# Attention block over 64 graphs: first group normed on VectorE, two-step weight scales, 11 warming matmuls, another order ahead of the loop

## The reference

```python
# x: 64 graphs x 128 tokens x 384, adj: 64 x 128 x 128 booleans, 6 heads of 64
h = jnp.maximum(_layernorm(x, axis=-1), 0.0)          # (x - mean) / sqrt(var + 1e-5), then ReLU
q, k, v = (_heads(h @ W + b) for W, b in ((Wq, bq), (Wk, bk), (Wv, bv)))
scores = jnp.einsum('bhqd,bhkd->bhqk', q, k) / np.sqrt(64)
bias = jnp.where(adj, 0.0, -9e15)[:, None]
probs = jax.nn.softmax(scores + bias, axis=-1)
ctx = jnp.einsum('bhqk,bhkd->bhqd', probs, v)
return x + ctx.transpose(0, 2, 1, 3).reshape(x.shape) @ Wf + bf
```

## Time and profile before

| | us |
|---|---|
| median of 3 runs | 475.55 |
| lowest, highest | 475.0, 476.55 |
| span of the profiled execution | 473.5 |
| PE busy, share of the span | 461.8, 98% |
| DVE, ACT, POOL busy | 369.9, 366.1, 303.6 |

### The profile page before, as it was taken

How to read it: one execution, slowest core, us unless ns; L and a number is a source line. 1 busy time by engine, 2 the same in 40 slices (tenths; PEclk the granted TensorE clock), 3 DMA queues, 4 the chain that set the end, 5 groups by cost and what they waited for, 6 DMA issues and landing times.

```text
span 473.5 us, 12912 instructions
## 1 busy us (share of the span) xinstructions
PE 461.8 (98%) x4457; PEld 273.0 (58%) x4457; DVE 369.9 (78%) x746; ACT 366.1 (77%) x820; POOL 303.6 (64%) x307
## 2 busy tenths in 40 slices
PE   7989999999999999999999999999999999999996
PEld 3645556556465565746556475665646556464763
DVE  5988979868888696886869688695987788687954
ACT  4879898876887887877788787788878877876950
POOL 3376767777678565767756576765667577533852
PEclk9999999999999999999999999999999999999999
DMA  8153959989979797896959679694969979776995
GB/s 302 61 118 90 162 112 169 187 182 215 187 138 225 118 194 175 184 199 124 215 123 213 155 156 214 130 213 80 217 147 164 239 120 163 184 108 150 150 192 162
DMA packets 219615, 78.56 MB, mean 166 GB/s; under 512 B 199472, under 2 KB 219568, under 8 KB 219568
## 3 DMA queue, kind: packets, MB, share of 16 engines
q1 hardware_dynamic: 209200, 65.63, 71.0%
q10 hardware_dynamic: 10368, 12.33, 9.6%
HBM read 16.19 MB, written 12.58 MB: 61 GB/s over the span
## 4 chain that ended last, share of the span: by engine, by line
PE 80%; DVE 6%; SPq 5%; issue 2%; POOL 2%; DMA 2%; ACT 2%; ACTq 0%; POOLq 0%; DVEq 0%
PE ps_proj L995 23%; PE ps_proj L997 22%; PE ps_proj L996 22%; PE ps_scores L1060 7%; SPq L565 2%; PE ps_ctx L995 2%; SPq L557 2%; PE ps_ctx L996 2%; PE ps_ctx L997 2%; PE ps_proj L1123 1%; DMA ht_parts<-h_pairs 1%; DMA ct_parts<-ctx_parts 1%; DVE shift_by L820 1%; POOL probs_parts L637 1%; DVE stats L807 1%
## 5 line engine op out<-in xcount | busy, mean ns | idle before, releaser
L637 POOL TENSOR_TENSOR probs_parts<-probs,probs_parts 128x768 f16<-128x768 f32 x64 | 105.3, 1646 | 35.2 <-ACT probs_parts L751 35.0
L736 ACT ACTIVATE probs<-masked,neg_max 128x128 f32<-128x128 f32 x384 | 118.5, 389 | 8.0 <-DVE neg_max L867 6.7
L995 PE MATMUL ps_proj<-ht_parts,w_hi 128*128 128x512 f16 (+1 forms) x309 | 109.8, 361 | 1.7 <-DVE qkt_lo L839 0.8
L996 PE MATMUL ps_proj<-ht_parts,w_hi 128*128 128x512 f16 (+1 forms) x309 | 109.7, 360 | 0.0
L997 PE MATMUL ps_proj<-ht_parts,w_lo 128*128 128x512 f16 (+1 forms) x309 | 109.7, 360 | 0.0
L720 ACT ACTIVATE qkt_hi<-ps_proj,bias_qk 128x512 f16<-128x512 f32 x94 | 63.6, 680 | 40.5 <-PE ps_proj L997 39.9
L643 POOL TENSOR_TENSOR ctx_parts<-ctx_sb,ctx_parts 128x384 f16<-128x384 f32 x62 | 56.9, 918 | 52.1 <-ACT ctx_parts L757 51.9
L839 DVE SCALAR_TENSOR_TENSOR qkt_lo<-ps_proj,bias_qk,qkt_hi 128x512 f16<-128x512 f32 x94 | 68.7, 740 | 22.0 <-ACT qkt_hi L720 22.0
L858 DVE SCALAR_TENSOR_TENSOR masked<-ps_scores,score_unscale,mask 128x384 f32<-128x384 f32 x128 | 72.5, 609 | 8.4 <-PE ps_scores L1060 8.4
L622 POOL TENSOR_TENSOR h_pairs<-h_sb,h_pairs 128x384 f16<-128x384 f32 x60 | 54.5, 917 | 37.6 <-ACT h_sb L711 37.5
L632 POOL TENSOR_TENSOR x_bf<-x_sb,b_out 128x384 f32<-128x384 f32 x64 | 63.1, 999 | 5.2 <-DVE y_sb L890 3.9
(11 more groups left out here) (102 smaller groups left out, 918.5 us busy)
## 6 DMA issues: line engine op xcount, KB each, us to landing
y<-y_sb SPq DMA_DIRECT2D x64, 192.0 KB, 2.6
x_sb<-in_x ACTq DMA_DIRECT2D x56, 192.0 KB, 3.2
x_sb<-in_x SPq DMA_DIRECT2D x8, 192.0 KB, 5.6
pt_parts<-probs_parts SPq DMA_TRANSPOSE x64, 4.0
ct_parts<-ctx_parts SPq DMA_TRANSPOSE x62, 3.0
adj_sb<-in_adj ACTq DMA_DIRECT2D x14, 64.0 KB, 2.8
w_raw<-in_Wk SPq DMA_DIRECT2D x1, 576.0 KB, 6.2
w_raw<-in_Wv SPq DMA_DIRECT2D x1, 576.0 KB, 7.3
```

Of the source, the lines that this page charges most:

```text
L637: nc.gpsimd.tensor_tensor(probs_parts[b][:, 1, :], probs[b % 2][:], probs_parts[b][:, 0, :], ALU.subtract).then_inc(probs_split, 1)
L736: last = nc.scalar.activation(probs[b % 2][:, u * N:(u + 1) * N], masked[b % 2][:, u, :], ACT.Exp, bias=neg_max[b % 2][:, u:u + 1])
L995: nc.tensor.matmul(to, a_hi, b_hi, start=first, stop=False)
L996: nc.tensor.matmul(to, a_hi, b_lo, start=False, stop=False)
```

## The change

- Group 0 is normed by DVE: one `tensor_scalar` per graph, (x - mean) * rstd in float32, SBUF to SBUF, in place of `first_shift` on DVE and `normalize_first` on ACT. The ReLU moves behind the transpose: `first_hi` takes `Relu` for `Copy`, and `first_lo` becomes a `scalar_tensor_tensor` (max with 0, minus hi). These instructions count on a semaphore of their own, `first_h_ready`.
- `scale` has two steps: the bound and the factor 1/1024 move into `sum_rows`, whose matrix holds 1/1024 and which adds one more matmul of a tiny constant (2 to the -100).
- `keep_busy` makes 11 matmuls at the start, not 15.
- All turns below 40000 are new, on all engines. The loop and what follows it keep their order. A few places of it:
  - DVE, start: statistics 0, reduce_bias, first_moments 0, reduce_first_rows 0 to 2, statistics 1, normalize_first 0, first_moments 1, scale 0, statistics 2 and 3, normalize_first 1, weight_rest 0, first_moments 2 and 3, first_lo 0, scale_bias 0, reduce_rows 0, normalize_first 2 and 3, weight_rest 1 and 2, first_lo 1, scale 1, reduce_rows 1, first_lo 2 and 3, statistics of group 1, scale 2, weight_rest 3, aggregate 1, weight_rest 4 to 6, shift 1, weight_rest 7 and 8, scale_bias 1, qk_lo 0, reduce_rows 2, score_unscale, additive_mask 0, qk_lo 1 to 3, scale 3, qk_lo 4 and 5, output_bias, values_lo 0 to 2, mask_scores 0, largest_score 0, mask_scores 1, statistics 2.0, largest_score 1, statistics 2.1 to 2.3, aggregate 2, values_lo 3, statistics 3.0 and 3.1, additive_mask 1, qk_lo 1.0.
  - PE, start: keep_busy, sum_rows 0, turn_first 0 and 1, keep_busy, keep_busy, turn_first 2, sum_rows 1, turn_first 3, first_q 0 and 1, sum_rows 2, first_q 2 and 3, project_qk 3 and 4, project_v 0, sum_rows 3, project_qk 5, project_v 1, project_bias, project_v 2, scores 0, project_v 3, project_qk 1.0 to 1.3, scores 0.1. Before: keep_busy, sum_rows 0, turn_first 0, keep_busy twice, turn_first 1, first_q 0, sum_rows 1, turn_first 2, first_q 1, sum_rows 2, turn_first 3, first_q 2 and 3, project_qk 3 to 5, sum_rows 3, project_v 0, project_bias, project_v 1 and 2, scores 0, project_v 3.
  - ACT: weight_hi 0 and 1, first_hi 0 and 1, weight_hi 2, first_hi 2 and 3, weight_hi 3 and 4, bias_term 0 to 2, weight_hi 5 to 8, qk_hi 0 and 1, normalize 1.0, qk_hi 2 and 3, normalize 1.1 to 1.3, qk_hi 4 and 5, values_hi 0 to 2; then the loads of x of groups 2 and 3 between exponentials.

```diff
-SCALE_STEPS = 3
+SCALE_STEPS = 2
-KEEP_BUSY = (15, 4, 3)
+KEEP_BUSY = (11, 4, 3)
...
-                nc.vector.tensor_scalar(w_bound[:, at], row_sum(n), TINY, 1.0 / ROWS_MOST, ALU.max, ALU.mult)\
-                    .then_inc(scale_step, 1)
+                nc.vector.tensor_scalar(w_unscale[:, at].bitcast(I32), row_sum(n).bitcast(I32), EXPONENT_BITS,
+                                        None, ALU.bitwise_and).then_inc(scale_step, 1)
                 dve.wait_ge(scale_step, before + 1)
-                nc.vector.tensor_scalar(w_unscale[:, at].bitcast(I32), w_bound[:, at].bitcast(I32), EXPONENT_BITS,
-                                        None, ALU.bitwise_and).then_inc(scale_step, 1)
-                dve.wait_ge(scale_step, before + 2)
                 nc.vector.reciprocal(w_scale[:, at], w_unscale[:, at]).then_inc(scale_step, 1)
...
-            def first_shift(group, n, i):
-                dve.wait_ge(rstd_ready, n + 1)
-                shift_graphs(0, first_parts[n])
+            def normalize_first(group, b, i):
+                at = slice(b, b + 1)
+                dve.wait_ge(rstd_ready, b + 1)
+                nc.vector.tensor_scalar(h_sb[:, b, :], x_sb[0][:, b, :], moments[0][:, b, 0:1], rstd[0][:, at],
+                                        ALU.subtract, ALU.mult).then_inc(first_h_ready, 1)
...
-                nc.vector.tensor_tensor(lo, first_turned(b), hi, ALU.subtract).then_inc(first_h_split, 1)
+                nc.vector.scalar_tensor_tensor(out=lo, in0=first_turned(b), scalar=0.0, in1=hi, op0=ALU.max,
+                                               op1=ALU.subtract).then_inc(first_h_split, 1)
...
+                nc.tensor.matmul(row_sum(n), parts_of_one[:], tiny[:], start=True, stop=False)
+                if n < 2:
+                    nc.tensor.matmul(row_sum(n), parts_of_one[:], bias_rows[:, n:n + 1], start=False, stop=False)
                 for c in range(C):
-                    last = nc.tensor.matmul(row_sum(n), ones[:], w_rows[:, n, c:c + 1], start=c == 0,
-                                            stop=n >= 2 and c == C - 1)
-                if n < 2:
-                    last = nc.tensor.matmul(row_sum(n), ones[:], bias_rows[:, n:n + 1], start=False, stop=True)
+                    last = nc.tensor.matmul(row_sum(n), parts_of_one[:], w_rows[:, n, c:c + 1], start=False,
+                                            stop=c == C - 1)
```

More of the change, by code:

```diff
@@ L66 @@
     0: {
[L67 to L82, removed]
-        "reduce_first_rows": (38390, 38400, 38420), "reduce_rows": (38570, 38610, 38780), "reduce_bias": (38430,),
@@ L126 @@
-    3: {
-        "load": (9090, 9100, 9200, 9210), "load_mask": (9400,), "statistics": (9110, 9210, 9240, 9290),
-        "aggregate": (9300,), "inverse_deviation": (9620,), "shift": (9310,), "normalize": (9320, 9410, 9420, 9430),
-        "normed_lo": (9650, 9680, 9710, 9720), "transpose_normed": (9740, 9760),
-        "project_qk": (9740, 9760, 9780, 9790, 9820, 9860), "qk_hi": (9600, 9620, 9650, 9670, 9720, 9790),
-        "qk_lo": (9600, 9670, 9680, 9710, 9760, 9800), "project_v": (9870, 9920, 9930, 9980),
-        "values_hi": (9830, 9880, 9930, 9960), "values_lo": (9830, 9900, 9940, 10223), "additive_mask": (9440,),
-        "residual": (9830, 9930, 9950, 9970), "scores": (9900, 9940), "mask_scores": (9840, 9850, 9910, 9990),
-        "largest_score": (9880, 9930, 9950, 10570), "exponentials": (9870, 9940, 9970, 12387),
-        "probs_hi": (9920, 9980, 11692, 14668), "probs_lo": (9980, 10460, 12021, 14997),
-        "transpose_probs": (9990, 11094, 12655, 15631),
-    },
@@ new lines @@
+        "qk_hi": (38760, 38770, 38790, 38800, 38840, 38850), "qk_lo": (38790, 38830, 38840, 38850, 38870, 38880),
+        "project_v": (39330, 39360, 39380, 39400), "values_hi": (38860, 38870, 38880, 38960),
+        "values_lo": (38900, 38910, 38920, 39020), "additive_mask": (38820,),
+        "residual": (39410, 39420, 39430, 39440), "scores": (39390, 39450),
+        "mask_scores": (38930, 38950, 39110, 39120), "largest_score": (38940, 38970, 39140, 39150),
+        "exponentials": (38980, 39020, 39180, 39190), "probs_hi": (39050, 39080, 39220, 39260),
@@ new lines @@
+    3: {
+        "load": (9000, 9010, 9070, 9250), "load_mask": (9200,), "statistics": (9030, 9040, 9130, 9270),
+        "aggregate": (9280,), "inverse_deviation": (9610,), "shift": (9310,), "normalize": (9360, 9370, 9380, 9450),
+        "normed_lo": (9660, 9670, 9700, 9720), "transpose_normed": (9720, 9770),
+        "project_qk": (9740, 9750, 9780, 9790, 9800, 9850), "qk_hi": (9600, 9640, 9680, 9690, 9710, 9770),
+        "qk_lo": (9600, 9620, 9690, 9710, 9780, 9790), "project_v": (9870, 9920, 9930, 9970),
+        "values_hi": (9810, 9840, 9880, 9940), "values_lo": (9840, 9890, 9900, 10223), "additive_mask": (9730,),
+        "residual": (9930, 9940, 9960, 9970), "scores": (9910, 9950), "mask_scores": (9850, 9870, 9920, 9980),
+        "largest_score": (9860, 9880, 9930, 10570), "exponentials": (9850, 9930, 9990, 12387),
+        "probs_hi": (9890, 9980, 11692, 14668), "probs_lo": (9950, 10460, 12021, 14997),
+        "transpose_probs": (9960, 11094, 12655, 15631),
+    },
```

151 lines of the change are left out of this document (84 added, 67 removed).

## The result

The changed kernel takes 472.34 us at the median of 13 executions (470.98 to 475.01), the kernel before 475.4 in the 13 between them: ratio 0.9932, 95% interval 0.9918 to 0.9946, so 3.1 us faster where 1.7 were forecast. The profiled span falls from 473.55 to 469.73 us.

| | first scores | first scores of the loop | last scores | end |
|---|---|---|---|---|
| before | 31.97 | 134.54 | 442.92 | 473.55 |
| after | 30.10 | 130.65 | 438.64 | 469.73 |
| difference | -1.87 | -3.89 | -4.28 | -3.82 |

A forecast was written before the change was run, and what follows sets the result against it. PE, 98% busy, was taken to bound the kernel. Terms of -2.16 us on DVE and PE's walk put the first scores 2.0 us earlier; 0.3 given back leaves -1.7: span 471.8, plus 2.05 around it, 473.85 us, range 472.3 to 475.9.

The forecast's parts named there:

- 0.3 given back: PE from the first scores to the loop: new gaps cost 0.3 us of the early gain, bounds -0.47 and +1.9.
- Scale in two steps: DVE ahead of the first scores: one dependent step of 0.19 us fewer, four times, -0.76 us.
- `first_shift` gone: DVE ahead of the first scores: four small independent instructions fall away, -0.3 us.
- The norm: DVE ahead of the first scores: four new norms, 0.35 us busy, a step of 0.27 each, +1.1 us, at most +1.85.
- `first_lo`: DVE ahead of the first scores: scalar_tensor_tensor at 611 ns against tensor_tensor at 551, four times, +0.24 us.
- The wait for the sums: DVE at the start: its 0.98 us idle for PE's weight row sums shrinks to about 0.1, -0.9 us.
- The shift of group 1: DVE ahead of the first scores: 0.94 us falls to 0.15 without POOL work beside it, -0.8; wait of 0.38 stays.
- The mask: DVE: additive_mask 1 moves behind the first scores, half of the two masks' 1.47 us, -0.74 us.
- PE beside it: PE's start walked: products from 12.5 us, 17.2 us of work, 0.2 of seams, first scores at 29.95 us.
- Given back behind the scores: Rival: behind the first scores, a late load of x makes DVE and PE 1.9 us late; 475.45 us, chance 0.22.
- The norm waiting for POOL: Rival: at the start, one DVE norm slowed by POOL beside it costs 0.75 us more; 474.6 us, chance 0.07.
- The clock: Rival: at PE's start the rise to 2.4 GHz comes late, half-rate work costs 3.25 us; 477.1 us, chance 0.09.

The follow-up runs named there:

- late_order: Kernel before with its own order up to the first scores and the changed kernel's order from there to the loop; 473.4 us, ratio 0.9942.
- three_steps_b: Changed kernel with scale back in three steps, second measurement; 471.61 us, ratio 0.9930.
- warm15: Changed kernel with 15 warming matmuls at the start in place of 11; 473.5 us, ratio 0.9940.
- before_warm11: Kernel before with 11 warming matmuls at the start in place of 15; 473.8 us, ratio 0.9985.
- after_again: Changed kernel itself, unedited, measured a second time; 472.51 us, ratio 0.9940.
- after_third: Changed kernel itself, unedited, measured a third time; 472.14 us, ratio 0.9924.
- early_only: Changed kernel with the order of the kernel before from the first scores to the loop; 475.05 us, ratio 0.9977.
- three_steps_end: Changed kernel with scale back in three steps and its extra buffer allocated behind all others; 473.08 us, ratio 0.9942.
- warm_no_second: Changed kernel without the 4 and 3 later warming matmuls; 474.19 us, ratio 0.9989.
- pad16: Changed kernel with an unused buffer of 16 bytes per partition and no added instruction; 472.09 us, ratio 0.9926.
- three_steps: Changed kernel with scale back in three steps, first measurement; 471.66 us, ratio 0.9906.

## Why the prediction was right, and where it was wrong

**What bounds it.** PE, before and after: right. That PE's idle time from 32.0 to 117.7 us was 0.47 us: this is the step that failed, and with it the term "0.3 given back", which starts from it; they carry the whole miss. The 0.47 was read off busy time, whose modelled ends hide up to 0.16 or 0.17 us of every hole, and the cut at 117.70 left out the largest hole, which lies at the loop's entry but is made by work issued ahead of it. By steps the same stretch, extended by one matmul, holds 2.0 us. The other half of the failed step is that the new order behind the scores was walked only up to the first weigh_values and credited with nothing; late_order shows that it brings 1.94 us by itself. "The loop and what follows it keep their order" was true and misleading: order ahead of the loop sets when its first operands land.

**The terms on DVE.**
- Scale in two steps, -0.76: 0.66 by three_steps_b at the first scores. Right.
- `first_shift` gone, -0.3: before, the four made steps of 0.06 to 0.08 us. Right.
- The norm, 0.35 us busy and a step of 0.27: mis-sized. It takes 0.46 with a step of 0.38 (6.44 to 6.82), and 0.86 for two, so +1.5 instead of +1.1, inside the stated bound of 1.85.
- `first_lo`, +0.24: nothing. The eviction with a ReLU takes 0.52 to 0.55 us, as the subtraction alone did (0.54, 0.55), with a step of 0.47; the 611 ns of the earlier trace rows is of a line that also reads and writes float32 in SBUF, and was the wrong row.
- The wait for the sums, -0.9: right; w_unscale is read at 6.91 (forecast 6.9, before 7.67 for the bound and 7.86) with no idle time ahead of it. warm15 and before_warm11 price the edit at 0.4 to 0.9.
- The shift of group 1: 0.16 us at 20.65 for 0.94, with a wait of 0.39 kept. Right on all three counts.
- The mask, -0.74: mis-sized. The two made a step of 1.40 before (26.43 to 27.83), the one that is left 0.35 (23.96 to 24.31): -1.05. Half of the 1.47 was no fair share, since a mask alone takes 0.43.
- Not in the sum: DVE idles 0.86 us for `qkt_hi` at 27.49. And in the kernel before a `w_lo` at 25.50 and a `bias_qk` at 24.53 took 1.01 and 0.39 us, while POOL ran `normed_lo`, for about 0.6 and 0.22 elsewhere: their steps are 0.6 us shorter now.

DVE is done with what the scores need, `values_lo` 0, at 29.28 + 0.55 = 29.83; the forecast was 29.75. That this comes out to 0.1 us is luck: +0.4 for the norm and +0.86 for the wait stand against -0.24, -0.3 and -0.6. The prediction had PE as the later of the two by 0.2 us. So it is in the first profile, where PE starts its products late (12.92). In after_again and after_third they start at 12.40, and PE waits for DVE in front of the scores, a hole of 0.4 us by steps. From after_again:

```profile
29.31 0.55 DVE L849 TENSOR_TENSOR v_lo<-ps_scores,v_hi 128x384 f16<-128x384 f32 x1
...
29.46 0.33 PE L1001 MATMUL ps_proj<-w_hi,ht_parts 128*128 128x384 f16 x1
30.01 0.23 PE L1064 MATMUL ps_scores<-qkt_hi 64*128 64x128 f16 x2 [0.22 <-DVE v_lo L849]
```

**The norm's rate.** The norm takes 0.46 us for 384 elements, 1.2 ns each; the mask 0.43 for 512, 0.84 ns; the plain three-operand form on 384, `w_lo`, 0.61. The Trainium skill, page "VectorE: DVE Perf Modes", section "The perf-mode tier table", gives fp32 tensor_scalar in SBUF twice the plain rate. By that rule the norm would be near the 0.35 forecast (my estimate); the mask agrees, the norm lies between the two rates. Whether its two scalars per partition, read from SBUF, make the difference wasn't tried. One pair of rows points that way: on a single element, a tensor_scalar with one such scalar (`score_unscale`) takes 0.20 us, one with immediates alone (`w_unscale` from SBUF, in the kernel before) 0.15.

**PE beside it.** turn_first 1 at 8.59 (8.5), turn_first 2 at 12.10 (11.3), first products at 12.92 (12.5), from there to the scores 17.18 us (17.2 of work and 0.2 of seams), first scores at 30.10, 30.01 and 30.03 in three executions (29.95). In the one profiled first, the seven warming matmuls ran at 1.2 GHz, which delays turn_first 2 by 0.6 against the two others (11.52) and costs under 0.1 at the scores, since those two lose the same time in waits for DVE. sum_rows 3 waits for nothing.

**Behind the scores.** values_lo 3 starts at 37.86 and ends at 38.39 (38.3): right, and PE waits only 0.3 us of a weight load for it. "0.3 given back, bounds -0.47 and +1.9": the truth is -2.0, outside both, since the lower bound was the misread idle time. With the right bound of -2.0, the same prediction would have run down to 473.85 - 2.3 - 0.8 = 470.75.

**The rivals.** Given back behind the scores (475.45): it did not happen in the changed kernel, but it is what early_only does, at 475.05 and by other waits (for `ctx_sb`, `ht_parts` and `pt_parts`, not for x). The new order is what keeps it away. The norm waiting for POOL: all four norms are alike (0.46, 0.46, 0.86 for two), it did not happen. The clock (477.1): the changed kernel's first profile has it at 1.2 GHz for a spell and pays nothing; three_steps_end has the rise as late as 14.2 us and pays 0.75, not the 3.25 of the sum: the rise comes with the first product, so none of the steady work runs at half rate (the 2.35 of the sum), and of the 1.5 us by which that product is later (14.19 for 12.68) half was lost before in the small waits that three_steps_b has; warm_no_second, with steady work at half rate for 3.9 us, pays 2.1.

**The ledger.** -1.9 at the first scores, -2.0 up to the loop, -0.4 where PE waits for `qkt_lo` near 410 us (a step of 1.13 is 0.74 after), and +0.5 in the last 31 us: -3.8 in the profiled spans, -3.1 between the medians. The 13 executions of each kernel spread over 3.5 and 4.0 us, and the profiled one of the changed kernel was a short one (471.44, the median 472.34).

## What to carry to other kernels

On an engine that is 98% busy, measure idle time by the steps between starts against the nominal step, never by busy time, and carry the stretch past the first wait of the loop: its operands are made by what stands ahead of it. An early gain is kept only if the chains behind it come earlier too; so price a change of order as a whole, at a mark far downstream, and not each wait by itself. When a start of some microseconds is tuned, take several profiles: loads, clock and tail move by as much as the edits.

## What the runs showed of the hardware that I had not expected

- With 11 warming matmuls the granted clock's path differs from one execution to the next. In after and pad16 the block takes 4.18 and 3.96 us (the rise comes before its end), the clock then falls back, and the second block runs at 1.2 GHz (2.98 and 2.75 us for 7); in after_again and after_third the first block takes 4.88, the second 1.67 at 2.4 GHz; in three_steps_end and three_steps 4.88 and 4.87, then 3.19. before_warm11 has the early rise too (3.91), but its second block starts at 7.03 already and keeps 2.4 GHz (1.67). In three_steps_end, the granted clock column says 1.00 for all stretches up to 17 us though the steps up to 14.2 are those of 1.2 GHz, as in the first microseconds of every kernel here: at the start, steps are to be read, not the column. Changed kernel, 9.2 to 11.8 us: 0.50 in after.
- The eight loads of x that open the kernel take 5.1 to 5.6 us from issue to landing at the median in three executions of the changed kernel and 7.1 in three_steps, issued at the same times (0.82, 1.74, 4.16). The statistics of graph 3 start at 8.88 there, at about 7.6 in the changed kernel, and the first scores differ by 1.3 us between three_steps and three_steps_b. How much of it is the loads and how much the low clock of three_steps can't be told; three_steps_end, with the clock alone, is 0.75 behind three_steps_b.
- PE's wait for the last transposed probabilities has its longest piece at 1.5 to 1.9 us or at 0.3 to 0.6 us, by whether the scale near the start has two steps or three, in all 16 profiles, with no effect on the time that could be told.
